# Softmax sums of a cross attention: exponentials added on VectorE and GpSimd before one ones multiply per group, with the groups reordered

## What is computed

```python
q = jnp.einsum('bsc,hcd->bhsd', xn, wq)      # xn: 4 x 256 x 128
k = jnp.einsum('btc,hcd->bhtd', yn, wk)      # yn: 4 x 1601 x 64
v = jnp.einsum('btc,hcd->bhtd', yn, wv)
a = jax.nn.softmax(jnp.einsum('bhsd,bhtd->bhst', q, k) * D ** (-0.5), axis=-1)
o = jnp.einsum('bhst,bhtd->bhsd', a, v)
```

## Time and profile before

| | us |
|---|---|
| median of 3 runs | 2724.49 |
| lowest, highest | 2718.17, 2734.19 |
| the profiled execution, its own time | 2717.35 |
| its span in the profile | 2715.6 |
| the 16 groups of `stage_cross`, from the first ST to the last division | 570 |

### The profile page before, as it was taken

One profiled execution on the slowest core, in us unless ns is written; L12 is line 12 of the kernel. 1 busy time (PEld: TensorE's weight loads), 2 busy tenths in 40 slices (PEclk: granted clock), 3 DMA queues, 4 the chain that ended last, 5 costly groups with the idle time before them and its releaser, 6 DMA issues. The chain is left out here.

```text
span 2715.6 us, 46818 instructions
## 1 busy us (share of the span) xinstructions
PE 2050.7 (76%) x17125; PEld 1118.7 (41%) x17125; DVE 1267.7 (47%) x2794; ACT 955.5 (35%) x1300; POOL 389.2 (14%) x334
## 2 busy tenths in 40 slices
PE   2853396989886299677999336743999999999498
PEld 1532261323334155424666203431455555555365
DVE  2842387778882333351443324534444444442322
ACT  1521161656663222102332113412244444444133
POOL 2110211000000000091111123410111111110100
PEclk7975596888998599797999667976699999999699
DMA  5428723132220001123221165301111111110010
GB/s 175 106 72 226 214 61 75 49 74 66 67 61 1 24 35 35 55 101 112 58 58 39 53 187 135 91 24 46 42 35 36 44 44 44 44 41 2 1 41 29
DMA packets 266743, 183.18 MB, mean 67 GB/s; under 512 B 27924, under 2 KB 252380, under 8 KB 265948
## 3 DMA queue, kind: packets, MB, share of 16 engines
q1 hardware_dynamic: 266588, 181.05, 24.3%
HBM read 92.20 MB, written 65.94 MB: 58 GB/s over the span
## 5 line engine op out<-in xcount | busy, mean ns | idle before, releaser
L1370 DVE TENSOR_REDUCE ta_mxp<-ps 128x1 f32<-128x401 f32 x512 | 267.1, 570 | 314.5 <-PE ps L1295 314.4
L784 DVE TENSOR_REDUCE ac_mxp<-ps 128x1 f32<-128x401 f32 x512 | 273.1, 567 | 44.6 <-PE ps L631 38.0
L1392 ACT ACTIVATE ta_prob<-ps 128x2048 f32<-128x2048 f32 (+1 forms) x112 | 196.6, 1755 | 147.3 <-PE ps L1331 147.3
L856 ACT ACTIVATE ac_prob<-ps 128x1024 f32<-128x1024 f32 (+1 forms) x208 | 210.2, 1024 | 106.0 <-PE ps L667 104.1
L631 PE MATMUL ps<-ac_kb,ac_qz 50*128 50x401 bf16 x512 | 181.9, 383 | 38.1 <-DVE ac_mxp L784 17.1
L784 DVE TENSOR_REDUCE a_mx<-ps 128x4 f32<-128x512 f32 (+1 forms) x160 | 106.9, 670 | 183.3 <-PE ps L635 153.0
L635 PE MATMUL ps<-a_kb,a_qb 64*128 64x256 f32 (+2 forms) x512 | 115.8, 336 | 57.7 <-DMA a_kb<-k 56.8
L1295 PE MATMUL ps<-ta_kb,ta_qb 96*128 96x401 bf16 x512 | 138.5, 354 | 17.9 <-DMA ta_kb<-ta_kh 12.1
L699 PE MATMUL ps<-ac_prob,ac_vs 128*32 128x256 f32 (+1 forms) x1664 | 147.1, 427 | 4.2 <-ACT ac_prob L856 4.2
L1327 PE MATMUL ps<-qxf,ta_k 32*128 32x256 f32 (+1 forms) x1664 | 133.6, 405 | 10.7 <-ACT ta_shiftT L1410 9.2
L1347 PE MATMUL ps<-ta_prob,ta_vs 128*32 128x256 f32 (+1 forms) x1664 | 131.5, 388 | 0.0
(11 more groups left out here) (290 smaller groups left out, 3411.6 us busy)
## 6 DMA issues: line engine op xcount, KB each, us to landing
ta_kb<-ta_kh SPq DMA_DIRECT2D x128, 100.1 KB, 2.2
vc<-c_vt SPq DMA_DIRECT2D x48, 256.0 KB
ac_vs<-vc SPq DMA_DIRECT2D x16, 768.0 KB
a_vs<-v SPq DMA_DIRECT2D x64, 128.0 KB
ac_kb<-kc SPq DMA_DIRECT2D x32, 200.1 KB, 3.5
ta_kb<-ta_kl SPq DMA_DIRECT2D x64, 100.1 KB, 2.2
ta_qb<-a1q SPq DMA_DIRECT2D x32, 192.0 KB, 2.9
ta_kb<-a1k SPq DMA_DIRECT2D x32, 192.0 KB, 3.7
```

Of the source, the lines that this page charges most:

```text
L784: v.tensor_reduce(o, i, AX.X, ALU.max).then_inc(scores_read.s, 1)
L856: a.activation(prob[0:rows, ring, 0:n], banks[0:rows, 0:n], ACT.Exp, scale=scale).then_inc(exp_done.s, 1)
L1370: v.tensor_reduce(mxp[:, qt * G + g, c:c + 1], k.ps[:, turns.bank(slot), 0:401], AX.X, ALU.max).then_inc(scores_read.s, 1)
L1392: a.activation(prob[0:rows, n % 2, :, 0:w], k.ps[0:rows, 2:6, 0:w], ACT.Exp, scale=scale).then_inc(exp_done.s, 1)
```

## The change

- **Sums.** The ones multiply of each tile goes. VectorE adds the exponentials of steps 1 and 2 into `acc[:, 0]` (`add_first`), GpSimd adds those of steps 3 to 7 into `acc[:, 1]` in four additions (`gather`), and VectorE adds the two (`add_rest`). One slot `sum` in the fourth step of the next group multiplies `acc[:, 1]` with ones (8 matmuls). Logarithm and reciprocal follow it.
- **Buffers.** `prob` has three buffers in place of two, and the exponential of a step waits until both the weigh and the addition of the step three before it are done.
- **Groups.** Group s is now head block s // 2 % 4 of batch s // 8 + 2 * (s % 2), so that neighbouring groups lie in opposite halves of the partitions. The key slots of group s + 2 and the value slots of group s + 1, which now have opposite halves, alternate in the first two steps.
- **Max slots.** They move from 6, 6, 5, 5, 5, 5, 0 to 4, 4, 6, 6, 6, 6, 0 per step.
- **Queries.** Their high and low parts go to DRAM once (two DMAs of 1 MB behind a block of their own), and a group fetches them with 3 DMAs in place of 12. Tile `yT` is allocated elsewhere.

```diff
-                if 0 <= s + 2 < groups and p < 4:
-                    late.append(("key", s + 2, p))
-                if 0 <= s + 1 < groups and 2 <= p < 6:
-                    late.append(("value", s + 1, p - 2))
+                for c in (2 * p, 2 * p + 1) if p < 2 else ():
+                    if 0 <= s + 2 < groups:
+                        late.append(("key", s + 2, c))
+                    if 0 <= s + 1 < groups:
+                        late.append(("value", s + 1, c))
+                if s > 0 and p == 3:
+                    late.append(("sum", s - 1, 0))
...
+                mixed = late + m
...
-MAX_AT = ((0, 6), (6, 12), (12, 17), (17, 22), (22, 27), (27, 32), (32, 32))
+MAX_AT = ((0, 4), (4, 8), (8, 14), (14, 20), (20, 26), (26, 32), (32, 32))
+ADD_AT = (9, 10)
...
+                for n, part in enumerate((high, low)):
+                    sp.dma_start(parts[n].rearrange("(j r) t -> r j t", j=4), part[:, :, :]).then_inc(loaded.s, 16)
+                sp.wait_ge(loaded.s, loaded.at(32))
...
     def half(s):
-        return slice(64 * (s // 8), 64 * (s // 8) + 64)
+        return slice(64 * (s % 2), 64 * (s % 2) + 64)
...
+                    elif kind == "sum":
+                        pe.wait_ge(added.s, added.at(2 * s + 2))
+                        for i in range(2):
+                            for g in range(G):
+                                ins = pe.matmul(bank[32 * g:32 * g + 32, 0:N], k.ones[:, 0:32],
+                                                acc[:, 1, g, i * N:(i + 1) * N], start=(i == 0), stop=(i == 1))
...
-                        for ones in (False, True):
-                            for g in range(G):
...
+                def add_first(s):
+                    n = s * STEPS
+                    v.wait_ge(exp_done.s, exp_done.at(n + 2))
+                    v.wait_ge(added.s, added.at(2 * s))
+                    v.tensor_tensor(acc[:, 0, :, :], prob[:, n % 3, :, :], prob[:, (n + 1) % 3, :, :],
+                                    ALU.add).then_inc(added.s, 1)
+                def add_rest(s):
+                    v.wait_ge(gathered.s, gathered.at(4 * s + 4))
+                    v.wait_ge(added.s, added.at(2 * s + 1))
+                    v.tensor_tensor(acc[:, 1, :, :], acc[:, 1, :, :], acc[:, 0, :, :], ALU.add).then_inc(added.s, 1)
                 for s in range(NS):
                     for n in range(32):
+                        if s > 1 and n == ADD_AT[0]:
+                            add_rest(s - 2)
+                        if s > 0 and n == ADD_AT[1]:
+                            add_first(s - 1)
...
-                    if n > 1:
-                        a.wait_ge(probs_used.s, probs_used.at(n - 1))
+                    if n > 2:
+                        a.wait_ge(probs_used.s, probs_used.at(n - 2))
+                        s0, p0 = divmod(n - 3, STEPS)
+                        if p0 < 2:
+                            a.wait_ge(added.s, added.at(2 * s0 + 1))
+                        else:
+                            a.wait_ge(gathered.s, gathered.at(4 * s0 + max(1, p0 - 2)))
...
+                def gather(s, p):
+                    n = s * STEPS + p
+                    g_.wait_ge(exp_done.s, exp_done.at(n + 1))
+                    rows, w = tile_rows(tiles_of(p)[-1]), N * len(tiles_of(p))
+                    if p == 3:
+                        if s > 0:
+                            g_.wait_ge(made.s, made.at(turns.made_at["sum", s - 1, 0] + 1))
+                        first = prob[:, (n - 1) % 3, :, :]
+                    else:
+                        g_.wait_ge(gathered.s, gathered.at(4 * s + p - 3))
+                        first = acc[0:rows, 1, :, 0:w]
+                    g_.tensor_tensor(acc[0:rows, 1, :, 0:w], first, prob[0:rows, n % 3, :, 0:w],
+                                     ALU.add).then_inc(gathered.s, 1)
                 for s in range(-2, NS):
                     if s + 2 < NS:
                         halves(s + 2)
+                    if s >= 0:
+                        gather(s, 3)
                     if s > 0:
                         divide(s - 1)
+                    if s >= 0:
+                        for p in range(4, STEPS):
+                            gather(s, p)
```

More of the change, by code:

```diff
@@ L1081, in __init__ @@
                 early, m = m[0:3], m[3:]
-                mixed = []
-                for a, b in itertools.zip_longest(late, m):
-                    mixed += [x for x in (a, b) if x is not None]
+                mixed = late + m
                 for when, some in ((0, early), (1, mixed)):
@@ L1090, in __init__ @@
                         table[slot] = len(table)
+        last = ("sum", groups - 1, 0)
+        self.reads.append(last)
+        self.made_at[last] = len(self.made_at)
         self.index = {slot: n for n, slot in enumerate(self.reads)}
@@ L1224, in stage_cross @@
     turns = Turns(NS, KT_CTX)
-    (scores, scores_read, made, taken, negmax, st_ready, exp_done, probs_used, out_read, logged, inverted, divided,
-     split, vec, filled) = (k.sems[n] for n in (
+    (scores, scores_read, made, taken, negmax, st_ready, exp_done, probs_used, out_read, inverted, divided,
+     split, vec, added, gathered) = (k.sems[n] for n in (
          "scores", "scores_read", "shift_t", "shift_in", "negmax", "st_ready", "exp_done", "probs_used", "out_read",
-         "act", "inverted", "divided", "pool", "vec", "filled"))
+         "inverted", "divided", "pool", "vec", "read", "masked"))
     ops = [k.sems["ops%d" % n] for n in range(2)]
-    NDMA = 24
+    NDMA = 15
     def tile_rows(t):
@@ L1253, in stage_cross @@
         vs = sb("vs", [P, 2, KT_CTX, P])
-        prob = sb("prob", [P, 2, G, 512])
+        prob = sb("prob", [P, 3, G, 512])
+        acc = sb("acc", [P, 2, G, 512])
         onesb = sb("onesb", [P, P], BF16)
@@ L1259, in stage_cross @@
         mx = sb("mx", [P, 2 * G])
-        sums = sb("sums", [P, 2, 2 * N])
+        sums = sb("sums", [P, 2, N])
+        logs = sb("logs", [P, N])
         inv = sb("inv", [P, 2, N])
@@ L1327, in transposed_scores @@
                             pe.matmul(k.ps[0:rows, 2 + g, (t % 2) * N:(t % 2 + 1) * N],
-                                      k32[r, s % 3, t * P:t * P + rows], q[r, s % 4, cols], start=True, stop=False)
+                                      k32[r, s % 3, t * P:t * P + rows], q[r, block_of(s), cols], start=True, stop=False)
                         for g in range(G):
@@ L1342, in weigh @@
                         rows = tile_rows(t)
-                        for ones in (False, True):
-                            for g in range(G):
-                                w = k.ones[0:rows, 0:32] if ones else vs[0:rows, s % 2, t, 32 * g:32 * g + 32]
-                                o = k.ps[32 * g:32 * g + 32, 6, N * ones:N * ones + N]
-                                ins = pe.matmul(o, w, prob[0:rows, n % 2, g, (t % 2) * N:(t % 2 + 1) * N],
-                                                start=(t == 0 and not ones), stop=(t == KT_CTX - 1), skip_group_check=True)
+                        for g in range(G):
+                            ins = pe.matmul(k.ps[32 * g:32 * g + 32, 6, 0:N], vs[0:rows, s % 2, t, 32 * g:32 * g + 32],
+                                            prob[0:rows, n % 3, g, (t % 2) * N:(t % 2 + 1) * N],
+                                            start=(t == 0), stop=(t == KT_CTX - 1))
                     ins.then_inc(probs_used.s, 1)
@@ L1381, in _ @@
                                            op0=ALU.mult, op1=ALU.subtract).then_inc(negmax.s, 1)
+                add_rest(NS - 2)
+                add_first(NS - 1)
+                add_rest(NS - 1)
             @block.scalar
@@ L1408, in take @@
                             "p (t c) -> p t c", c=P), ACT.Copy)
+                    elif kind == "sum":
+                        ins = a.activation(logs[:, :], bank[:, 0:N], ACT.Ln)
                     else:
@@ L1411, in take @@
                     ins.then_inc(taken.s, 1)
+                    if kind == "sum":
+                        a.wait_ge(taken.s, taken.at(turns.made_at[slot] + 1))
+                        a.activation(inv[:, s % 2, :], logs[:, :], ACT.Exp, scale=-1.0).then_inc(inverted.s, 1)
                 def results(s):
@@ L1431, in _ @@
                 results(NS - 1)
+                take(("sum", NS - 1, 0))
             @block.gpsimd
```

65 lines of the change are left out of this document (40 added, 25 removed).

## The result

The changed kernel takes 2789.83 us (median of 4 runs, 2786.52 to 2808.02), the kernel before, in the same session, 2725.66 (4 runs, 2718.17 to 2734.19). The ratio is 1.025, with a 95% interval of 1.0206 to 1.0293: slower by 64 us, where the forecast was 150. The time lies inside the range, close to rival A (2785).

The account below looks back on a forecast made before the run. TensorE was taken as the bound. A group's terms 29.0 + 4.5 + 3.0 + 4.7 + 4.2 gave 45.5 us against 36.28; 13 groups +120, with the ends +151: 2875 us, range 2710 to 2910.

Parts of the forecast that it names:

- rival A: Only the third-step port wait; line 1378 does not contend, 1380 is served first; group 38.9 us, total 2785; chance 0.22.
- first place: Third step: VectorE's addition waits for GpSimd's split of k, which holds the shared port; +3.0 us a group.
- second place: Negated maxima before the shift: line 1380 waits for a GpSimd addition on the port; +4.7 us a group.
- steps without waits for VectorE's additions: TensorE's steps of one group without any wait: 29.0 us against 36.28 before.
- hold by VectorE's additions: Third step: TensorE waits for maxima queued behind VectorE's two additions; 8.1 us in place of 3.55, +4.5 a group.
- clock: TensorE idles in third and last step, granted clock halves; 4.2 us at half, 2.1 lost each; +4.2 a group.
- 0.3 us decide: Argument against rival A, at the negated maxima: whether line 1380 is served first hangs on 0.3 us.
- Rival B: Additions hold TensorE in the third step, the port does not: 2699, chance 0.12; with clock lost 2729, chance 0.09.
- Pairing: Key and value projections in opposite row halves overlap on TensorE: -1.5 of 7.1 us a group, bounds 0 and -3.5.
- The ends: Outside the 13 steady groups: first group +2 us, second last +9, last +10, queries' DMAs +10.
- C: As meant: TensorE bound at 29.0 us a group, with VectorE ahead at reduction 9; total 2640; chance 0.03.

Follow-up runs that it names:

- the small additions: Changed kernel with GpSimd's splits waiting for `add_first`, each VectorE addition covering one column of each head instead of 512, other sums left out; 2649.35 us.
- the later splits: Changed kernel with GpSimd starting the two splits of k only when `add_first` is done; 2763.63 us, ratio 1.0134.
- the clock kept: Changed kernel with unread bf16 matmuls behind max slots 11 and 12, so TensorE works while it would wait; 2749.98 us, ratio 1.0106.
- the division last: Changed kernel with GpSimd dividing behind its last addition of the group, not between the first and second; 2944.2 us, ratio 1.0807.
- the pairing alone: Changed kernel with ones multiplies back, no additions or sum slot, two `prob` buffers; new order and queries in DRAM stay; 2682.45 us, ratio 0.9854.
- old order: Changed kernel with keys in steps 1 to 4, values in steps 3 to 6 and maxima spread as before; 2864.78 us, ratio 1.0528.
- the earlier additions alone: Changed kernel with VectorE's additions ahead of reductions 7 and 8 instead of 9 and 10, splits not waiting; 2686.59 us, ratio 0.982.

## Why the prediction was wrong in size, and what was right in it

The bound, the sign and the first place were right: TensorE waits between max 11 and max 12 because the additions stand ahead of reductions 9 and 10, and the first of them waits for GpSimd. The second place was wrong, and the spell of half clock that was to follow it: 4.7 + 2.1 us a group, 88 us of the 150 that were forecast. Of the terms of the group:

| term (us a group) | forecast | measured | by |
|---|---|---|---|
| steps without waits for VectorE's additions | 29.0 | 29.46 | the small additions |
| hold by VectorE's additions | +4.5 | +4.3 | what is left of 39.3; 4.07 by its waits |
| port, first place | +3.0 | +2.4 | the later splits (39.3 to 36.9) |
| port, second place | +4.7 | +0.3, within the first line | the changed kernel |
| clock | +4.2, two spells | +3.1, one spell | the clock kept (39.3 to 36.2) |
| sum | 45.5 | 39.3 | |

The hold is what the other terms leave, so the measured column adds up by itself.

The step that failed is the **second place**: "the third addition is next in line, and 1380 waits 4.5 us". It rests on when the negated maxima ask. The forecast had that as 9.6 us after the sum with GpSimd's addition ending at 9.9, and the trace has 9.3 and 9.8 (2279.62 and 2280.07 behind a sum made at 2270.3), so it was right to 0.3 us. What it had not counted is that GpSimd takes 0.14 us from one instruction to the next, and that line 1378 (1431 now) ends 0.04 us after the port is free; line 1380 (1433) is then served before GpSimd: in all 16 groups it takes 0.19 to 0.20 us. The nearest row was the cast, which says that the wait exists, and it does, once in this very trace: line 1431 over the 16 groups (durations min/median/max in ns), and the shift from which the second group, of 46.83 us, is counted.

```profile
L1431 DVE TENSOR_SCALAR ta_negm<-ta_mx x16: 184/488/3953, 1952.4 to 2550.3; 128x8 bf16<-128x8 f32 x16
```

```profile
1997.63 0.41 PE L1348 MATMUL ps<-identb,ta_negm 128*32 128x128 bf16 x8 [4.10 <-DVE ta_negm L1433]
```

With the division last, line 1433 takes 4.40 to 4.42 us in 14 of 16 groups. So the prediction's "0.3 us decide" was true, and here they decide against the wait.

The **clock** term was too small for each spell and too large in number. Half clock was to last 4.2 us a spell, from the earlier trace rows (6 us and 3.5). It lasts 10.2 us in the third and fourth steps, and 17.1 after the second place's wait in the changed kernel's second group, whose first two steps take 7.0 us more than in the steady ones. Two spells of 2.1 were counted; there is one, worth 3.1. Had the second place occurred, the forecast of 2875 would have been 69 us low, as the run with the division last shows (2944): two errors that partly hid each other. Rival B left open whether the hold of the additions alone loses the clock. It does, with 1.73 and 2.34 us of waiting (the later splits).

**First place**: `add_rest` was to ask 2.2 us after the third ST and get the port at 5.2; it asks at 2.18 and `kl` ends at 4.97. **Pairing**: -1.5 of 7.1 was forecast, with -3.5 as the bound. Four keys and four values take 2.62 + 2.02 = 4.6 us in the changed kernel, so -2.5, and -3.3 in the group of the run with the pairing alone, where the maxima are moved too. The claim that the next key starts only behind the last value pass is wrong: in the changed kernel the second key of a step starts beside the last matmuls of the first value (both at 2250.68 in the group above). The Trainium skill, "TensorEngine Tiling (Array Packing)", Theoretical Speedup, allows up to 2x; 7.1 to 4.6 is 1.5x. By that figure the prediction put the sum 2.0 us lower than its own; it was 1.0 lower.

**Steps without waits**: 29.0 was nearly met by two errors. The first two steps take 10.6 us and not 11.2, by the better pairing. The last takes 3.29 and not 2.6: 0.7 was taken off for the ones multiplies, but TensorE then stands before the shift 0.65 us early, since VectorE needs that long for its last reduction and the small instructions. In the group of before TensorE came last there, by which the wait could not be seen.

**The ends.** Tail +12.4 (forecast +10); the queries' DMAs +7.4 (+10), as from the start of their matmuls to the first projection it is 21.1 us against 13.75. Filling the pipeline then takes 5.7 us less than before, which the forecast lacked. The second last group, +9 forecast, has only +3.3: it has no second place either. First group +3.0 (+2).

**Rival A** has the time: 38.9 a group and 2785 us forecast, 39.3 and 2790 measured. It had 0.22. Its reason is wrong, though. It said that line 1378 does not contend, and the line does wait for GpSimd (0.49 us for 0.18, and once 3.95); the wait is short only because GpSimd's addition is about to end. And its number is close by luck in part, with the port at 2.4 where it had 3.0 and the clock at 3.1 where it had 2.1. **Rival B** (the port doesn't hold) is refuted by 4.93 against 2.28 us for one size. **C** needed VectorE ahead of TensorE at reduction 9. It is not at 9 and 10, but nearly so at 7 and 8, because the projections stand beside them: 30.3 us a group. The prediction looked at this place only for what it costs, not for the neighbour that would cover it.

The Trainium skill, "SBUF — State Buffer", Who interferes with whom, says that the port pair which VectorE shares with GpSimd is an exclusive lock, and that issue order decides who blocks. The trace agrees, in both directions (4.93 us for VectorE's 2.28, 4.94 for GpSimd's 3.02).

## What to carry to other kernels

Ask what TensorE has queued beside a long instruction on a helper engine: the same two additions cost 6.7 us of waiting ahead of reductions 9 and 10, and ahead of 7 and 8 1.3, or 0.4 where GpSimd's splits wait too. Where two engines share a port and one of them works in long instructions, a wait of 4 us can hang on 0.1 us of timing; price such a place as either nothing or all of it, look in the trace for a group in which it did go wrong, and keep short critical instructions away from it. And price an idle spell of TensorE with what it does to the clock: here that was 3.1 us for 6.7 of waiting, and 3.6 to 7.0 for 4.6.

## What the runs showed of the hardware

- Between two queued GpSimd instructions that share the port there are 0.14 us. A VectorE instruction that already waits gets in there, and a short one behind it too (2280.14 before 2280.21); one that asks 0.13 us after the next has started waits for all of it (4.41 us for 0.19).
- An instruction of 8 columns with one SBUF input (line 1431, float32 to bf16) waits for the port like a large one (3.95 us for 0.18), and so does one with two (line 1433). Reductions did not: from PSUM 0.57 us beside a running GpSimd instruction, and from SBUF (line 1426) 0.19 us in all 16 groups, as in the kernel before.
- Half clock lasts far longer than the idle that comes before it. With TensorE busy it ended after 10.2 us (changed kernel), 13.7 (small additions; old order) and 17.1 (division last); in the earlier trace rows after 3.5 to 6. It began behind two idle pieces of 4.38 and 2.34 us, or 1.73 and 2.34, with one max slot between them. But it also began in one group with nothing longer than 0.77 and 0.58 around the shift, where eight others with such waits kept full clock, and at a wait of 1.34 us in some groups of the run with the earlier additions alone and not in others. What tells them apart is not shown.
- A key and a value projection in opposite halves of the rows start within 10 ns of each other and run side by side: four keys and four values take 4.6 us in place of 7.1.
